# A second gate tile moved ahead of the left-over activation, adapter pieces spread one per output tile, and two more output tiles ahead of the rank products in a fused fp32 layer kernel

## The reference, cut to what matters

```python
# x is 32 batches of 64 tokens by 1024 channels, float32
h  = einsum('bct,bcd->bdt', x, W[itok_0_15])                 # token mixing, one 64x64 matrix per batch
x1 = x + (h @ W_base.T + b_base) + 0.5 * irfft(masked low-rank product of h).sum(experts)
# gated feed-forward with one LoRA adapter (rank 16) per batch, F = 2752
gate = x1 @ W_gate.T + 0.5 * (x1 @ A_gate[i].T) @ B_gate[i].T
up   = x1 @ W_up.T   + 0.5 * (x1 @ A_up[i].T)   @ B_up[i].T
act  = silu(gate) * up
down = act @ W_down.T + 0.5 * (act @ A_down[i].T) @ B_down[i].T
out  = x1 + down @ sign(weight).T + bias
```

## Time and profile before

| | before |
|---|---|
| median of 3 runs | 2011.75 us |
| the profiled execution | 2011.54 us, of which the span is 2009.8 us |
| PE busy | 1967.8 us (98%) |
| DVE busy | 1488.9 us (74%) |
| ACT busy | 760.0 us (38%) |
| POOL busy | 539.1 us (27%) |
| TensorE clock granted | 0.994 of full speed on average |

### The profile page before, as it was taken

The page is one execution under the profiler, slowest core; times in us unless marked ns, Lnnn a source line. Parts: engine busy times, 40 slices in busy tenths (PEclk is TensorE's granted clock), DMA queues, the critical chain, the costliest instruction groups (busy, mean ns, idle before and its releaser), DMA issues.

```text
span 2009.8 us, 33180 instructions
## 1 busy us (share of the span) xinstructions
PE 1967.8 (98%) x9232; PEld 1641.0 (82%) x9232; DVE 1488.9 (74%) x2464; ACT 760.0 (38%) x1434; POOL 539.1 (27%) x932
## 2 busy tenths in 40 slices
PE   7999999999999999999999999999999999999998
PEld 5878888887887888888798788888879788888876
DVE  6578777777758777777766777777866787777785
ACT  3243333333334333333334443333324543334330
POOL 5232222212413222221521422222070322222000
PEclk8999999999999999999999999999999999999999
DMA  9455555542456544454244745454324755555411
GB/s 248 116 120 117 117 114 108 116 93 64 114 116 134 113 105 103 107 116 101 64 127 109 155 105 114 104 108 106 84 64 126 149 117 117 107 115 116 88 22 42
DMA packets 320447, 219.21 MB, mean 109 GB/s; under 512 B 177080, under 2 KB 311096, under 8 KB 320352
## 3 DMA queue, kind: packets, MB, share of 16 engines
q1 hardware_dynamic: 282848, 189.67, 41.2%
q0 software_dynamic: 36352, 24.19, 7.1%
q10 hardware_dynamic: 1152, 4.19, 0.5%
HBM read 205.07 MB, written 12.58 MB: 108 GB/s over the span
## 4 chain that ended last, share of the span: by engine, by line
PE 82%; DVE 8%; issue 4%; ACT 4%; DMA 1%; SPq 1%; DVEq 0%; POOLq 0%; ACTq 0%; POOL 0%
PE ps L1258 22%; PE ps L1260 22%; PE ps L1259 22%; PE ps L1448 6%; DVE ps L806 3%; PE ps L1381 2%; PE ps L1308 2%; PE ps L1309 2%; DVE split L792 1%; PE ps L1475 1%; PE ps L1284 1%; ACT split L564 1%; ACT lora_b L537 1%; PE ps L1282 1%; DVE ps L867 1%
## 5 line engine op out<-in xcount | busy, mean ns | idle before, releaser
L1258 PE MATMUL ps<-x,split 128*128 128x512 f32 x1440 | 564.1, 392 | 12.7 <-DVE split L792 10.2
L1260 PE MATMUL ps<-x,split 128*128 128x512 f32 x1440 | 561.9, 390 | 0.0
L1259 PE MATMUL ps<-x,split 128*128 128x512 f32 x1440 | 561.1, 390 | 0.0
L564 ACT ACTIVATE split<-ps 128x512 fp32r<-128x512 f32 x360 | 213.9, 599 | 459.3 <-DVE ps L806 459.0
L469 POOL DMA_DIRECT2D nat_ad<-L_cond_A_down x224 | 137.0, 618 | 744.4 <-DVE ps L806 733.8
L1258 PEld LDWEIGHTS ps<-x,split 128*128 128x128 f32 x1440 | 271.3, 188 | 67.4 <-issue 12.2
L1260 PEld LDWEIGHTS ps<-x,split 128*128 128x128 f32 x1440 | 270.7, 188 | 58.6
L1259 PEld LDWEIGHTS ps<-x,split 128*128 128x128 f32 x1440 | 270.7, 188 | 57.2
L792 DVE TENSOR_TENSOR split<-ps,split 128x512 fp32r<-128x512 f32 (+1 forms) x392 | 253.9, 686 | 14.1
L1258 PE MATMUL ps<-hidden 128*128 128x512 f32 x672 | 262.1, 390 | 0.0
L1259 PE MATMUL ps<-hidden 128*128 128x512 f32 x672 | 261.7, 389 | 0.0
(11 more groups left out here) (118 smaller groups left out, 2720.9 us busy)
## 6 DMA issues: line engine op xcount, KB each, us to landing
nat<-L_cond_W_gate SPq DMA_DIRECT2D x336, 128.0 KB
nat<-L_cond_W_up SPq DMA_DIRECT2D x336, 128.0 KB
nat_down<-L_cond_W_down SPq DMA_DIRECT2D x112, 384.0 KB, 6.4
nat_a<-L_ffn_weight SPq DMA_DIRECT2D x96, 128.0 KB, 2.8
nat<-effective_weight SPq DMA_DIRECT2D x24, 512.0 KB
nat<-x SPq DMA_DIRECT2D x16, 512.0 KB
nat_b<-L_cond_B_gate POOLq DMA_DIRECT2D x224, 24.0 KB, 2.5
nat_b<-L_cond_B_up POOLq DMA_DIRECT2D x224, 24.0 KB, 2.4
```

Source lines behind the costliest of these rows:

```text
L564: act.activation(dst, src, func).then_inc(piece_hi, 1)
L1258: pe.matmul(dst, a[0], b[0], start=first, stop=False)
L1259: pe.matmul(dst, a[0], b[1], start=False, stop=False)
L1260: return pe.matmul(dst, a[1], b[0], start=False, stop=last)
```

## The change: what it does

It has four edits. `HEAD` and the orders of DVE, ACT and SP's waits change together.

1. Unit G1 moves from behind S6, S7 and `act_rest` to right behind unit U0; the small down adapter ADREM follows it, then `act_rest`, then S6 and S7. ACT's copy of G1's high part now waits for `rest_read`, a new semaphore that PE raises when REM's own matmuls are done, since it takes REM's slot of `split` while REM's adapter product is still ahead.
2. In the first layer of groups 2 to 4 the pieces B go one each to tiles 2, 3 and 4: transposed ahead of the weight's low part, finished behind it.
3. At a group's end PE does two thirds of tile 3 with tile 2 ahead of the last activation, and whole tiles 4 to 7 instead of 3 to 5 ahead of `last_products`. `bank_read` waits for the bank's last user instead of for tile i - 2.
4. SP's waits for the slots of U1, G2 and U2 follow the new order: in part 0 for S6, S7 and G1, in later parts for the tile that held the slot. Part 0 of SP's loop is written out for that.

SP's loads keep their order: G0, U0, S6, S7, G1, the sign tile into `nat_a`, U1, G2, U2, nextG0.

```diff
 HEAD = (["B"] * 3 + ["AG"] * 2 + ["AU"] * 2 + ["REM"] * 2 + ["BREM"] + ["G0"] * 2 + ["U0"] * 2
-        + ["ADREM"] + ["S6"] * 2 + ["S7"] * 2 + ["G1"] * 2)
+        + ["G1"] * 2 + ["ADREM"] + ["S6"] * 2 + ["S7"] * 2)
...
                 if n >= NAT_GU + 3:
-                    name = ("nextB", "nextU0", "nextG1", "U1", "G2", "U2")[n - NAT_GU - 3]
-                    c = first_of(name) + (3 if name == "nextB" else 2)
-                    if n < NAT_GU + 6:
-                        c -= PART_PIECES
-                    sp.wait_ge(piece_turned, piece_number(g, q, c))
+                    name = ("nextG0", "nextU0", "nextG1", "U1", "G2", "U2")[n - NAT_GU - 3]
+                    if n >= NAT_GU + 6:
+                        sp.wait_ge(piece_turned, piece_number(g, q, first_of(name) + 2))
+                    elif isinstance(q, int) and q == 0:
+                        sp.wait_ge(piece_turned, piece_number(g, 0, first_of(("S6", "S7", "G1")[n - NAT_GU - 3]) + 2))
+                    else:
+                        sp.wait_ge(piece_turned, piece_number(g, q - 1, first_of(name) + 2))
...
                 elif m == SPLIT_REM + 3:
-                    act.wait_ge(rest_psum, g + 1)
+                    act.wait_ge(rest_read, g + 1)
...
                 unit(g, 0, "U0", SPLIT_GU + 1)
+                unit(g, 0, "G1", SPLIT_GU + 2)
                 c = first_of("ADREM")
...
+                act_rest(g)
                 sign_unit(g, 0, "S6", 6)
                 sign_unit(g, 0, "S7", 7)
-                act_rest(g)
-                unit(g, 0, "G1", SPLIT_GU + 2)
...
                     if u < 5:
+                        if not making and u >= 2:
+                            if u == 2:
+                                dve.wait_ge(x1_sum, 8 * g + 2)
+                                dve.wait_ge(nat_b_full, 256 * (NQ * g + 1))
+                            lora_b_turn(g, 0, "B", u - 2)
                         if making:
                             made_unit(3 + u)
                         else:
                             first_weight_unit(g, 3 + u)
-                        if u == 4:
+                        if not making and u >= 2:
+                            lora_b_low(g, 0, "B", u - 2)
+                        if making and u == 4:
                             dve.wait_ge(x1_sum, 8 * g + 2)
                             lora_b_tiles(g, 0, "B", 0)
...
                 weight_unit(g, 0, "U0", NAT_FIRST[1], SPLIT_GU + 1)
+                weight_unit(g, 0, "G1", NAT_FIRST[2], SPLIT_GU + 2)
                 a_down_rest(g)
+                act_rest(g)
                 sign_unit(g, 0)
                 sign_unit(g, 1)
-                act_rest(g)
                 dve.wait_ge(out_stored[0], 64 * (START + g))
-                weight_unit(g, 0, "G1", NAT_FIRST[2], SPLIT_GU + 2)
...
                 def bank_read(i):
 
-                    pe.wait_ge(down_added, ADDED + DOWNS * g + STAGE * q + max(0, i - 2))
+                    user = max((n + 1 for n in range(i) if banks[n] == banks[i]), default=0)
+                    pe.wait_ge(down_added, ADDED + DOWNS * g + STAGE * q + user)
...
                 tiles(2, (0, 1))
+                pe.wait_ge(up_read, START + ACTS * g + PT * q + 3)
+                tiles(3, (0, 1))
                 pe.wait_ge(act_lo, START + ACTS * g + PT * q + 4)
                 for half in range(2):
                     ranks(half, (2,), False)
                     ranks_rest(half).then_inc(down_psum, 1)
-                tiles(2, (2,), False)
+                for i in (2, 3):
+                    tiles(i, (2,), False)
                 pe.wait_ge(up_read, START + ACTS * (g + 1))
-                for i in (3, 4, 5):
+                for i in (4, 5, 6, 7):
+                    bank_read(i)
                     tiles(i, range(PT), False)
                 pe.wait_ge(piece_lo, START + LOW_PIECES * (g + 1))
                 pe.wait_ge(rank_lo, START + 3 * g + 3)
-                for i in (2, 3, 4, 5):
+                for i in range(2, 8):
                     last_products(i)
-                for i in range(6, STAGE):
+                for i in (8, 9):
```

More of the change, by code:

```diff
@@ L210, in build_layers @@
         ranks_added, ranks_moved, ranks_whole = sem("ranks_added"), sem("ranks_moved"), sem("ranks_whole")
-        rest_psum, rest_moved = sem("rest_psum"), sem("rest_moved")
+        rest_read, rest_psum, rest_moved = sem("rest_read"), sem("rest_psum"), sem("rest_moved")
         gate_psum, up_psum = sem("gate_psum"), sem("up_psum")
@@ L345, in load_down_rest, with load_part @@
                       .then_inc(nat_down_full, 16)
+            def load_part(g, q):
+                load_sign_part(g, q)
+                for k in range(3, 6):
+                    load_gate_up(g, q, NAT_GU + k, q, k)
+                for k in range(2):
+                    load_gate_up(g, q, NAT_GU + PART_UNITS + k, q + 1, k)
+                sp.wait_ge(piece_turned, piece_number(g, q, first_of("D2") + 2))
+                load_down(q + 1)
+                load_gate_up(g, q, NAT_GU + PART_UNITS + 2, q + 1, 2)
             def group(g):
@@ L359, in group @@
                 load_gate_up(g, 0, NAT_FIRST[2], 0, 2)
[L360 to L368, removed]
+                load_part(g, 0)
+                with sp.Fori(1, NQ - 1) as q:
+                    load_part(g, q)
                 for k in range(3, 6):
@@ L591, in down_tile, with lora_b_tiles @@
                           bank_of(c + half).rearrange("p (m h) -> p m h", m=4))
-            def lora_b_tiles(g, q, name, part):
+            def lora_b_tiles(g, q, name, part, js=range(PT)):
                 c = first_of(name)
                 act.wait_ge(up_psum, START + TILES * g + PT * part)
-                for j in range(PT):
+                for j in js:
                     doubled(g, q, c + j, [lora_b[:, kind, j].rearrange("p t f -> p (t f)") for kind in range(2)],
@@ L730, in first_layer_all @@
                             weight_unit(g, 3 + u)
-                        if u == 4:
[L732 to L735, removed]
+                        if making and u == 4:
+                            act.wait_ge(plain_lo, 12)
+                            for v in range(KC):
+                                act.wait_ge(w_stored[v], 16)
                             lora_b_tiles(g, 0, "B", 0)
+                        if not making and u >= 2:
+                            lora_b_tiles(g, 0, "B", 0, (u - 2,))
                     else:
@@ L916, in a_down_tiles, with lora_b_turn, lora_b_low @@
                           bank_of(c)[:, 0:PT * P].rearrange("p (j h r) -> p j h r", j=PT, h=2), lora_ad[:, :, 0::3, :])
+            def lora_b_turn(g, q, name, j):
+                c = first_of(name) + j
+                rows = nat_b[:].rearrange("p t fq s (j r) -> p j (t fq) r s", j=PT)
+                turn(g, q, c, bank_of(c)[:, 0:256].rearrange("p (n r s) -> p n r s", n=8, r=RANK), rows[:, j])
+            def lora_b_low(g, q, name, j):
+                c = first_of(name) + j
+                doubled_low(g, q, c, [lora_b[:, kind, j].rearrange("p t f -> p (t f)") for kind in range(3)],
+                            bank_of(c)[:, 0:256])
             def lora_b_tiles(g, q, name, part):
-                c = first_of(name)
                 dve.wait_ge(nat_b_full, 256 * (NQ * g + part + 1))
[L921 to L925, removed]
                 for j in range(PT):
-                    turn(g, q, c + j, bank_of(c + j)[:, 0:256].rearrange("p (n r s) -> p n r s", n=8, r=RANK), rows[:, j])
+                    lora_b_turn(g, q, name, j)
                     if j > 0:
-                        low(j - 1)
-                low(PT - 1)
+                        lora_b_low(g, q, name, j - 1)
+                lora_b_low(g, q, name, PT - 1)
             def lora_b_rest(g):
@@ L1330, in gate_up_rest @@
                 pe.wait_ge(rank_sum, 3 * g + 1)
-                of_x1(ps[:, 2, :], SPLIT_REM, False)
+                of_x1(ps[:, 2, :], SPLIT_REM, False).then_inc(rest_read, 1)
             def gate_up_rest_adapter(g):
```

## The result

The changed kernel takes 2021.49 us (median of 6 runs, 2018.1 to 2022.85), the kernel before 2011.68 beside it (6 runs). The ratio is 1.0047, 95% interval 1.0036 to 1.0058: slower by 0.5%. The profiled execution took 2022.85, its span 2021.1, against 2011.54 and 2009.8. It was the slowest of the six, so the two profiles lie 11.3 us apart and the medians 9.8.

A forecast was written before the change was run, and what follows sets the result against it. PE, busy 98% of the span, bounds the kernel, but DVE sets the pace in the head. From 2011.54 us, -7.3 at the group's end and +19.6 in the head, with DVE's lead counted there, give 2023.8, 2024 us; range 2018 to 2031.

The forecast's parts named there:

- The group's end: PE's waits for the last activation tile and the rank products' low part go: 1.83 us per group, -7.3 in all.
- The B pieces: Spread over three first-layer tiles, they let DVE start tile 7 1.98 us earlier in groups 2, 3 and 4.
- T: The start of G1's transpose on DVE in a head; 614.5 forecast in group 2.
- The loads: In the head, G1's load takes 4.5 us and U1's 5.0 from first issue; DVE starts 0.45 after landing.
- S6 free at T + 8.4: In the head, S6's slot, which U1's load needs, is released 8.4 us after G1's transpose starts.
- The price of the head: Slot waits on DVE delay U1 by +6.4, +4.7, +4.1 and +4.4 us in groups 1 to 4, together +19.6.
- That the two waits add up: In the head, DVE's waits for G1's and U1's loads both delay U1, within the +19.6 us.
- only G1's wait is real: Rival: U1's load is there when S7 is done, so U1 starts at T + 9.7; 2007 us, chance 0.07.
- U1 to nextG0 stays 24.9: In the head, from U1's transpose on DVE to PE's start of nextG0 stays 24.9 us.
- PE's brackets: PE waits 5 to 8 us at U1, about 1.5 at nextG0, none at G1 or the group's end.
- The clock pays too: Rival: PE's waits in the heads slow its clock, costing 4 × 1.5 = 6 us more; 2030, chance 0.12.
- Loads short: Rival: the head's loads take 3.6 us in place of 4.5 and 5.0, near no change; 2014.6, chance 0.08.

The follow-up runs named there:

- the mended head order: Edits 1 to 3, loads in order of use, sign tiles ahead of `act_rest`, B_down gathered behind U0's tile, against the kernel before: 1998.3 us, 0.9934.

## Why the prediction was right, and where it was not

- **The forecast**: 2024 (2018 to 2031), measured 2021.49. The case was the likeliest one: both slot waits are real and DVE's lateness at U1 goes through to PE. DVE's idle stretches were 2.6 to 2.9 us ahead of G1 and 3.2 to 3.7 ahead of U1, where about 3 to 4 and about 4 were named.
- **The group's end** (-7.3 predicted): -8.3 in the profile, and 8.3 between the medians in the run with this edit alone. The waits went as the prediction put it. The term was sized 0.25 too low per group, since a matmul chain that starts behind a wait also loses about 0.1 in its first matmuls (the first rank product took 0.85 before and 0.74 in the version with this edit alone, the first `last_products` 0.81 and 0.71), and two tiles that now lie in the plain row are 0.03 shorter each.
- **The B pieces** (1.98 us of DVE's lead in groups 2 to 4): this step failed. The prediction took the loop's turn for unchanged and the lead for free to travel into T. DVE does leave the first layer 1.8 us sooner in all three groups, but at U0's transpose 0.7, 0.3 and 1.8 us are left of it in groups 2, 3 and 4. In groups 2 and 3 the turn grew from 1.2 to 3.0 and 2.8 us and the clock fell behind it, and DVE needs AG's result before it comes to G1; group 4 has no turn there. Alone the edit brings nothing (0.9992). The mechanism is that POOL's gathers of B_down are released by AG's transposes, which DVE now does 4.6 us earlier against PE, in the middle of the W_down load. Taking them away brought the turn back to 1.3; the 6.8 us on DVE under W_down show from the other side that a turn is longer beside traffic.
- **The loads** (4.5 and 5.0 us from first issue, 0.45 more to DVE): 4.00 to 4.15 and 4.41 to 4.87 in the four groups, and DVE starts at most 0.2 after the landing. Both terms were too high: T lay 4.0 to 4.3 after the issue and not 4.95, U1 4.6 to 5.1 after its issue and not 5.45.
- **S6 free at T + 8.4**: 627.20 + 1.3 - 619.97 = 8.5. Right, and SP's issue at 628.53 with it.
- **The price of the head** (+19.6): 18.7 in the profiles, 19.6 between medians with edit 2 and 3 in both. Per head it is 6.3, 4.5, 4.7 and 3.2, where 6.4, 4.7, 4.1 and 4.4 were forecast. The agreement is partly luck: the two loads cost 1.1 to 1.6 us less per head than assumed, against 1.3 and 1.7 of DVE's lead that did not arrive in groups 2 and 3, and 1.3 of slow clock in group 1. In group 4 nothing stands against it, and the forecast is 1.2 too high.
- **That the two waits add up**: not a term of the sum, but the reading of it. The prediction lets G1's whole delay go into T and on to U1. The runs show that of the 2.6 to 2.9 us only 0.4 to 0.9 per head count (1.7 to 3.6 in all). A DVE that comes sooner waits for REM's product instead. The rival "only G1's wait is real" (2007) has its run in the one with G1's load held, 2006.1.
- **U1 to nextG0 stays 24.9**: 658.07 - 633.12 = 24.95, and 24.9 in groups 3 and 4. In group 1 it is 26.2: the clock was down for 6.8 us there, more than PE's spare.
- **PE's brackets**: 3.70 to 4.41 at U1 and none at nextG0, where 5 to 8 and about 1.5 were named. DVE's start of U1 came sooner than assumed, in groups 2 and 3 PE came later by the turn and the slow clock behind it, and what was to be left at nextG0 went into the fall of the clock behind U1.
- **"The clock pays too"** (2030, 0.12): the falls came in every head, so by its own test the forecast was wrong there, but not the price of those behind U1. One fall of 3.4 us costs PE 1.7 us, and PE had 1.7 us to spare ahead of nextG0, as the prediction had worked out for one. The Trainium skill's warning (TensorE: Matmul & The Clock Gate, section Why this matters for your kernels) holds for the clock in all four groups (3.9 to 4.6 us lost at U1). On the time, of the falls behind U1 only group 1's longer one shows; those behind AG in groups 2 and 3 are part of the lead that was lost.
- **"Loads short"** (2014.6): it asked for loads of 3.6 us. G1's were 0.4 to 0.5 us shorter than the prediction's term and U1's 0.1 to 0.6, together about a third of what it asked.

## What to carry to other kernels

When a tile is moved forward in an order of work, move its load and its slot in the same way, and ask of every wait that appears which other wait it covers: here one of the two slot waits cost under 1 us per head and the other 3 to 4. When an edit makes an off-path engine earlier, look at what its semaphores release and what is just then in flight; a gather that started 5 us sooner lengthened another engine's loop turn. Time a compound change in parts: here one part gained 8 us, one nothing, and one lost 19.6. Then time the mended version against the one without the part: here the mended head order was no faster than the old one.

## What the runs showed of the hardware

- A hardware loop's turn costs time by what the DMA engines do. On PE: 0 and 0.16 us with the engines idle ahead of it, 1.1 to 1.5 us when the W_down load ends 1.5 to 2 us ahead of F7's last matmul, 2.7 to 3.2 when it, or the gathers behind it, end in the last microsecond. On DVE, where it does not wait for PE: 2.6 to 3.8 us, and 6.8 under a 1.5 MB load. In every version PE starts AG 3.0 to 3.6 us behind the start of the instruction packet, also with idle engines, where the packet begins 2.7 to 2.8 us ahead of F7's last matmul and the time is all but covered. I read it as the fetch standing behind data packets. What orders the packets in the engines is not shown.
- In the heads the clock fell behind all 19 waits on PE in which 2.99 us or more were lost, and behind some of 2.5 to 3.0: it did at 2.53, 2.75, 2.83 and 2.96, and did not at 2.56, 2.71, 2.79 and 2.97. The length of the wait alone does not decide there. What does, I did not try.
- The same kernel's runs spread by 0.8 to 6 us here (2006.31 to 2012.32 for the B pieces alone). That spread fits falls of the clock that come or stay away: the three fastest of the B pieces' eleven runs have a mean granted clock of 0.995, the others 0.992 and 0.993. But only the profiled runs show the clock over time, so it stays open.
